# The causal mask of the turned scores: two products on TensorE, or a select by GpSimd on the exponentials

## What is computed

```
q = Q @ WQ + bQ ; k = K @ WK + bK ; v = V @ WV + bV        # 16 heads of 16
scores = einsum('bhqd,bhkd->bhqk', q, k) * SCALE
scores = where(causal, scores, -inf)
probs = softmax(scores, axis=-1)
out = einsum('bhqk,bhkd->bhqd', probs, v) ... @ WO + bO
x = x + out
```

## Time and profile before

| what | value |
|---|---|
| time, median of 3 executions | 732.27 us (730.75 to 733.64) |
| time of the profiled execution | 739.06 us |
| span of the profiled execution | 737.3 us, 11898 instructions |
| busy, share of the span | PE 85%, PEld 70%, DVE 68%, ACT 48%, POOL 45% |
| mean granted TensorE clock | 0.898 of 2.4 GHz |
| chain that ended last, by engine | PE 39%, issue 6%, DVE 5%, POOL 5%, DMA 4%, SP queue 4%, ACT 1% |

### The profile page before, as it was taken

One profiled execution on the slowest core, in us unless ns is written; L12 is line 12 of the kernel. 1 busy time (PEld: TensorE's weight loads), 2 busy tenths in 40 slices (PEclk: granted clock), 3 DMA queues, 4 the chain that ended last, 5 costly groups with the idle time before them and its releaser, 6 DMA issues.

```text
span 737.3 us, 11898 instructions
## 1 busy us (share of the span) xinstructions
PE 626.5 (85%) x4100; PEld 518.1 (70%) x4100; DVE 501.1 (68%) x1066; ACT 350.2 (48%) x683; POOL 333.7 (45%) x322
## 2 busy tenths in 40 slices
PE   3586998997987688889989851799999999999992
PEld 2465887876875554556555531799999999999992
DVE  5687688787696546666657262387888888788841
ACT  4565464662543024352343421356666666666551
POOL 1234424224240032112143367344868677686776
PEclk9798999999999669997788665699999999999997
DMA  9201403775317926556365410704263452521223
GB/s 295 83 3 43 128 29 89 274 203 139 90 44 198 211 64 164 133 141 163 83 162 142 160 38 17 254 22 152 25 170 68 127 153 43 168 31 17 28 29 44
DMA packets 63315, 81.64 MB, mean 111 GB/s; under 512 B 10295, under 2 KB 47938, under 8 KB 63256
## 3 DMA queue, kind: packets, MB, share of 16 engines
q1 hardware_dynamic: 53928, 72.85, 35.2%
q0 software_dynamic: 9216, 7.81, 7.4%
q10 hardware_dynamic: 112, 0.23, 0.1%
HBM read 48.27 MB, written 34.36 MB: 112 GB/s over the span
## 4 chain that ended last, share of the span: by engine, by line
PE 39%; issue 6%; DVE 5%; POOL 5%; DMA 4%; SPq 4%; ACT 1%; POOLq 0%; DVEq 0%; ACTq 0%
PE l_scores L101 13%; PE w_bank L1765 13%; DMA l_lo<-kd 3%; POOL out L1418 2%; PE a_out L1621 2%; SPq L208 2%; PE a_shared L1641 2%; POOL disp L1387 2%; PE l_scores L1699 2%; PE a_turned L1603 1%; PE l_scores L1722 1%; PE a_turned L1589 1%; PE l_scores L261 1%; DVE w_yt L1966 1%; DVE l_nm L275 1%
## 5 line engine op out<-in xcount | busy, mean ns | idle before, releaser
L1954 DVE SCALAR_TENSOR_TENSOR w_v<-w_th,l_scores 128x324 f32<-128x324 f32 x128 | 62.1, 490 | 55.1 <-ACT w_th L1509 53.8
L1509 ACT ACTIVATE w_th<-l_scores 128x324 f32<-128x324 f32 x128 | 56.4, 441 | 84.7 <-PE l_scores L101 83.8
L1405 POOL TENSOR_TENSOR l_lo<-w_v,l_hi 128x324 fp32r<-128x324 f32 x64 | 59.0, 922 | 75.0 <-ACT l_hi L1515 74.8
L1470 ACT ACTIVATE a_pr<-a_turned 128x1024 f32<-128x1024 f32 x48 | 49.1, 1023 | 89.1 <-PE a_turned L1603 87.2
L101 PE MATMUL l_scores<-l_hi,w_w1h 128*128 128x324 f32 x256 | 81.1, 317 | 2.3 <-DVE l_lo L1946 1.2
L1418 POOL DMA_INDIRECT out<-w_y,w_to x48 | 76.3, 1591 | 12.1 <-issue 9.7
L101 PE MATMUL l_scores<-l_lo,w_w1h 128*128 128x324 f32 x256 | 80.6, 315 | 0.0
L101 PE MATMUL l_scores<-l_hi,w_w1l 128*128 128x324 f32 x256 | 80.5, 314 | 0.0
L275 DVE TENSOR_REDUCE l_nm<-l_scores 128x4 f32<-128x1024 f32 (+1 forms) x48 | 58.3, 1215 | 31.7 <-PE l_scores L261 30.9
L1765 PE MATMUL w_bank<-l_hi,w_w2h 128*128 128x324 f32 x256 | 64.5, 323 | 2.2 <-DVE w_yt L1966 1.2
L1515 ACT ACTIVATE l_hi<-w_v 128x324 fp32r<-128x324 f32 x128 | 59.9, 472 | 12.4 <-DVE w_v L1954 11.7
(11 more groups left out here) (253 smaller groups left out, 1587.0 us busy)
## 6 DMA issues: line engine op xcount, KB each, us to landing
w_s<-in_L_ffn_w SPq DMA_DIRECT2D x14, 1024.0 KB, 7.4
l_lo<-kd SPq DMA_DIRECT2D x32, 200.0 KB
l_hi<-qd SPq DMA_DIRECT2D x32, 192.0 KB
disp<-c_blank SPq DMA_DIRECT2D x8, 658.1 KB
w_rows<-disp SPq DMA_DIRECT2D x7, 658.1 KB
kd<-l_qkh SPq DMA_DIRECT2D x16, 256.0 KB, 4.7
vd<-m_vf SPq DMA_DIRECT2D x4, 1024.0 KB, 6.8
qd<-l_qkh SPq DMA_DIRECT2D x16, 256.0 KB, 3.9
```

The source lines that it names most:

```text
L1405: pool.tensor_tensor(hl[:, g % 3, half(1)], v[:, n % 4, :], hh[:, g % 3, half(1)].bitcast(F32), ALU.subtract)\
L1470: act.activation(pr[n % 3][:, :], tbank[:, :], ACT.Exp, scale=SCALE).then_inc(A["exp"], 1)
L1509: act.activation(th[:, n % 2, :], hb[n % 2][:, 0:HALF], ACT.Tanh, scale=0.5).then_inc(F["th"], 1)
L1954: dve.scalar_tensor_tensor(v[:, n % 4, :], th[:, n % 2, :], 1.0, hb[n % 2][:, 0:HALF], ALU.add, ALU.mult).then_inc(F["v"], 1)
```

## The change

`turned_mask` is gone from TensorE and with it 2 products for each of 48 items. `turned(n)` now writes `a_turned` afresh (start=True) and itself waits for the exponential of item n - 1. The exponentials of keys after the query are then not zero, and GpSimd sets them to zero in SBUF: `cut(n)` is an affine select over the diagonal blocks of `pr`, 4 x 128 columns for s = 0 and 1, and 8 x 128 (all of the tile) for s = 2. `weigh(n)` waits for `cut(n)` in place of the exponential. The bias is added by tiles of 256 columns, one behind each of `cut(0)` to `cut(15)`; the additions of `base` become tiles too, one in each of steps 22 to 25 and 34 to 37, and eight at the end. Waits on their semaphores count tiles.

```
@@ -1317,7 +1317,7 @@
                                  .rearrange("(p t) d -> p t d", t=ST)).then_inc(F[f"rows{e % 2}"], 16)
 
                 def store_base(i):
-                    sp.wait_ge(S["base"], i + 1)
+                    sp.wait_ge(S["base"], TPB * (i + 1))
                     sp.dma_start(out[i * BLK:(i + 1) * BLK, :].rearrange("(t p) d -> p t d", p=P),
                                  x_sb[:, i * TPB * D:(i + 1) * TPB * D].rearrange("p (t d) -> p t d", d=D))\
                         .then_inc(S["based"], 16)
@@ -1357,19 +1357,23 @@
 
             @block.gpsimd
             def _(pool):
-                def with_bias(i):
-                    m = x_sb[:, i * TPB * D:(i + 1) * TPB * D].rearrange("p (t d) -> p t d", d=D)
-                    pool.tensor_tensor(m, m, bo[:, :].unsqueeze(1).to_broadcast([P, TPB, D]), ALU.add).then_inc(S["xb"], 1)
+                def with_bias(t):
+                    pool.tensor_tensor(tile(x_sb, t), tile(x_sb, t), bo[:, :], ALU.add).then_inc(S["xb"], 1)
 
                 def power(i):
                     _, own, nt = tiles(i)
                     pool.wait_ge(S["ve"], i + 1)
                     pool.tensor_tensor(rstd[:, own], ve[:, own], c["mhalf"][:, 0:nt], ALU.pow).then_inc(S["rstd"], 1)
 
-                def base(i):
-                    pool.wait_ge(S["x3"], TPB * (i + 1))
-                    m = x_sb[:, i * TPB * D:(i + 1) * TPB * D].rearrange("p (t d) -> p t d", d=D)
-                    pool.tensor_tensor(m, m, x3[:, i * TPB:(i + 1) * TPB, 0:D], ALU.add).then_inc(S["base"], 1)
+                def base(t):
+                    pool.wait_ge(S["x3"], t + 1)
+                    pool.tensor_tensor(tile(x_sb, t), tile(x_sb, t), x3[:, t, 0:D], ALU.add).then_inc(S["base"], 1)
+
+                def cut(n):
+                    pool.wait_ge(A["exp"], n + 1)
+                    own = pr[n % 3][:, :].rearrange("k (m q) -> k m q", m=8 if n % 3 == 2 else 4)[:, :, 0:P]
+                    pool.affine_select(out=own, in_=own, compare_op=ALU.is_ge, fill=0.0, base=0,
+                                       pattern=[[0, own.shape[1]], [1, P]], channel_multiplier=-1).then_inc(A["cut"], 1)
 
                 def divide(g):
                     pool.wait_ge(A["po"], 2 * g + 2)
@@ -1422,15 +1426,18 @@
 
                 pool.iota(x3[:, :, TOK:TOK + 1].bitcast(U32), [[P, NT], [1, 1]], base=0, channel_multiplier=1)\
                     .then_inc(S["xb"], 1)
-                for i in range(NBLK):
-                    with_bias(i)
                 for t in range(END):
+                    if t < NS:
+                        cut(t)
+                    if t < NT:
+                        with_bias(t)
                     if t % 3 == 0 and 1 <= t // 3 <= GR:
                         divide(t // 3 - 1)
                     for i in units(t, "power"):
                         power(i)
-                    if t in BASE:
-                        base(BASE.index(t))
+                    for i, first in enumerate(BASE):
+                        if first <= t < first + TPB:
+                            base(TPB * i + t - first)
                     if t % 6 == 3 and 1 <= t // 6 < FC:
                         low_w1(0, t // 6 - 1)
                     if t % 6 == 0 and 1 <= t // 6 < FC:
@@ -1441,8 +1448,8 @@
                                 scatter(i, n)
                 low_first_w2(FC - 1)
                 low_w1(0, FC - 1)
-                base(NBLK - 2)
-                base(NBLK - 1)
+                for t in range(TPB * (NBLK - 2), NT):
+                    base(t)
                 low(0)
                 for e in range(E):
                     for f in range(FC):
@@ -1580,16 +1587,8 @@
 
                     return [(p, e) for p in range(4) for e in range(2) if s == 2 or p // 2 == s]
 
-                def turned_mask(n):
+                def turned(n):
                     ge(pe, A["exp"], n)
-                    for e in range(2):
-                        bank = tbank[:, e * 4 * P:(e + 1) * 4 * P]
-                        m = 4 if n % 3 == 2 else 2
-                        out = bank.rearrange("k (p q) -> k p q", p=m)[:, :, 0:P]
-                        pe.matmul(out, c["mask"][:, :], c["identb"][:, :].unsqueeze(1).to_broadcast([P, m, P]),
-                                  start=True, stop=False, skip_group_check=True)
-
-                def turned(n):
                     g, s = divmod(n, 3)
                     if s == 0:
                         pe.wait_ge(A[f"m_in{g % 2}"], 32 * (g // 2 + 1))
@@ -1600,14 +1599,14 @@
                         key = slice(P, L) if s == 2 else slice(0, P)
                         w = P if s == 2 else L
                         at = e * 4 * P + (p if s == 2 else p % 2) * w
-                        mm = pe.matmul(tbank[:, at:at + w], kx[rows, p, key], q[rows, p, tok], start=False, stop=True,
+                        mm = pe.matmul(tbank[:, at:at + w], kx[rows, p, key], q[rows, p, tok], start=True, stop=True,
                                        skip_group_check=True)
                     mm.then_inc(A["st"], 1)
 
                 def weigh(n):
                     g, s = divmod(n, 3)
                     b, k = divmod(g, 2)
-                    pe.wait_ge(A["exp"], n + 1)
+                    pe.wait_ge(A["cut"], n + 1)
                     if s == 0:
                         ge(pe, A["po"], 2 * g - 1)
                         pe.wait_ge(A[f"v_in{b % 2}"], 16 * (b // 2 + 1))
@@ -1769,8 +1768,6 @@
 
                 for t in range(END):
                     u = t + LEAD
-                    if t < NS:
-                        turned_mask(t)
                     if u < NS:
                         mask(pe, A, c, lead, u)
                     if t < NS:
@@ -1847,7 +1844,7 @@
                     dve.transpose(ot[:, k, (b % 2) * L:(b % 2 + 1) * L], on[:, :]).then_inc(A["o"], 1)
 
                 def x2(b):
-                    dve.wait_ge(S["xb"], b // 2 + 2)
+                    dve.wait_ge(S["xb"], 2 * b + 3)
                     dve.wait_ge(S["y"], b + 1)
                     m = x_sb[:, 2 * b * D:(2 * b + 2) * D]
                     dve.tensor_tensor(m, y_bank(b)[:, :], m, ALU.add).then_inc(S["x2"], 1)
```

11 lines of the change are left out of this document (4 added, 7 removed).

## The result

| kernel | time, median | ratio to before, 95% interval | mean granted clock |
|---|---|---|---|
| before | 732.48 us (730.75 to 733.64, 4 runs) | | 0.898 (the profiled one, 739.06 us) |
| after | 759.39 us (758.57 to 762.36, 4 runs) | 1.0377 (1.034 to 1.0413) | 0.856 (the profiled one) |

The change makes the kernel 27 us slower. 730.8 us was predicted, with 723.5 to 738 as the range: wrong in sign and in size. The profiled execution of after took 760.13 us, with a span of 758.4. From the fetch of the second expert's rows to the end of the span it is 278.2 us before and 278.0 after, so everything was lost in attention with routing. The execution whose profile serves as before in the rows took 739.06 us and is none of these four.

A forecast was written before the change was run, and what follows sets the result against it. The laying loop, and TensorE when its clock is low, were taken to bound the attention stage in turn. Terms -7.1 + 1.6 + 3.0 + 1.0 = -1.5 us took 739.06 to 737.6 us, carried to 730.8 against the median; range 723.5 to 738.

The forecast's parts named there:

- The additions by tiles ... I count nothing: GpSimd: splitting four additions of 2.36 us into sixteen quarters costs nothing, 0.5 us either way.
- the three rivals: Alternatives: faster, no added clock loss (0.34); slower by clock in the laying loop (0.18); slower by GpSimd's queue (0.08).
- Masks in a full TensorE: -7.1: Attention stage, three stretches where TensorE bounds: masks removed there save 7.1 us (5 to 10); the other 32 count nothing.
- clock falls in two loop turns: +3.0: Laying loop: longer waits for keys lower TensorE's clock, slowing the projection by 1.5 us in each of two turns.
- Rival 2: Laying loop: lower clock slows three turns, costing 9.0 us instead of 3.0; slower, 736.8 us; chance 0.18.
- Shared port: +1.0 (0 to 3): VectorE's small operations on the maxima wait while GpSimd's cuts hold the shared port: 1.0 us more.
- The cuts are hidden: Mid-stage: cuts of 0.7 and 1.2 us finish before `weigh` needs them, if GpSimd is free when the exponential ends.
- a sign of being wrong: Mid-stage: TensorE waiting for cuts for more than 2 us in sum would count against the prediction.
- Rival 3: GpSimd's queue: cuts at upper price (1.17 and 2.35 us) delay steps and the end; about 736.8 us; chance 0.08.
- Tail cut: +1.6: Stage end: the cut before `weigh(46)` queues behind power, low part and scatter, delaying the turned normed rows by 1.6 us.

The follow-up runs named there:

- tiles_only: The kernel before with only the additions of the normed rows by tiles; masks stay products, no cuts: 750.87 us, ratio 1.0295.
- products_gone: The kernel before without the 96 `turned_mask` products, so the turned scores get no causal mask; all additions whole: 736.98 us, ratio 1.01.
- bias_tiles: The kernel before with only the bias added by tiles in the first 16 steps: 731.33 us, ratio 0.9991.
- cut_aside: The kernel before plus 48 GpSimd selects of the cuts' shapes on their own SBUF tile, results awaited by nobody: 736.08 us, ratio 1.0072.
- both_masks: base_whole with the 96 mask products put back on TensorE, overwritten by the turned scores: 736.20 us, ratio 1.0083.
- cut_only: products_gone with the cuts on GpSimd; bias and normed rows added whole: 745.95 us, ratio 1.0226.
- base_whole: The kernel after with the additions of the normed rows whole again; cuts and bias by tiles stay: 744.26 us, ratio 1.024.

## Why the prediction was wrong

- **The step that failed most: "The additions by tiles ... I count nothing".** I asked where GpSimd had room for the additions, and when they began, but not who waits for the last one and what stands behind that waiter. It is SyncE, with the maxima's store and the next keys behind it. The changed wait of `store_base` stood in the diff, and its place ahead of the next group's store in SyncE's loop stood in the kernel. The prediction had this term at 0 with 0.5 us either way. tiles_only priced it at 21 us alone; taking it out of after gave back 15 and 16 us by the medians (10 and 9 by the ratios). None of the three rivals was this one.
- **"Masks in a full TensorE: -7.1", and "clock falls in two loop turns: +3.0".** Taken together these gave -4.1 us; products_gone, which does just this, measured 1.0% or 7 us slower (0.57 to 1.43%, 4 to 10 us). The -7.1 rested on the earlier trace rows: products leave a TensorE that bounds. Those rows are of the execution of 739.06 us. In bias_tiles, nearer to the median, the same 15 us are nearly all at the high clock:

```profile
342.00:357.00 15.00, 14.36 (x152) 8.83 (x150) 12.36 (x39) 5.94 (x8) 2.61 (x4) 0.94 0.46 110
```

  And the granted clock isn't fixed. With fewer products more of the stage runs at 1.2 GHz (0.75 against 0.87 above), and the products left take longer. I had priced only a projection in two turns behind a wait. Rival 2 had the right direction: its -7.1 and +9.0 make +1.9 us for this edit alone, where 7 were measured. That its total of 736.8 us is also the time of products_gone is chance, since it counts 2.6 us for the cuts, which products_gone hasn't. The Trainium skill, page "TensorE: Matmul & The Clock Gate", section "HAM oscillation — how this bites in real kernels", which the prediction cites, says that waits for a DMA bring the clock down, so that the next burst starts slow. The trace of products_gone agrees in one place: TensorE waits 1.86 us for the keys of 333.98, and the straight mask took 0.60 us (two products of 512 columns) before the wait, while the projection of 334.99 behind it took 3.78 us. The projection of 314.95 is slow without a wait in front of it; the clock was at 0.50 from 309 us on, with TensorE busy throughout. The prediction gave low clock of both kinds too little weight.
- **"Shared port: +1.0 (0 to 3)".** The hold-up is there as described, but the term was too small: running the selects costs 0.72% or 5.3 us (3 to 7.6) in cut_aside, if not all of it through these operations. I took half of 0.4 us for each of the turns; measured are 0.31 us (cut_aside) and 0.50 us (both_masks) for each of 16 groups in these two operations alone.
- **"The cuts are hidden".** Nearly right in the middle of the stage: 0.64 and 1.10 us each, and TensorE's wait for them was 2.9 us in six places up to 440 us in after, above the 2 us that the prediction had named as a sign of being wrong. The cuts took 37.9 us in all; the lower bound of that sum is 38 us, not the 36 that the prediction has. Rival 3, GpSimd's queue with cuts at their upper price, fell by the measured lengths. cut_aside shows besides that the selects cost about as much when nobody waits for them.
- **"Tail cut: +1.6".** In after the cut of item 46 stands behind the power, the low part and a scatter, as the earlier trace rows had let expect:

```profile
447.49 1.05 POOL L1391 DMA_INDIRECT disp<-w_x,w_si  x1 [0.18 <-issue]
448.56 0.65 POOL L1375 TENSOR_SCALAR_AFFINE_SELECT a_pr<-a_pr 128x512 f32<-128x512 f32 x1
```

```profile
449.26 1.08 PE L1620 MATMUL a_out<-a_pr,l_lo 128*32 128x256 f32 x8 [3.56 <-POOL a_pr L1375]
```

  `weigh(46)` came 4.5 us after the end of its exponential (444.74) instead of 1.2. The turned rows at 450.28 couldn't have begun before ScalarE had the normed rows at 448.46, so at most 1.8 us of it counts, and the stretch from the last exponential to the last scatter grew from 27.9 to 29.9 us. The prediction's 1.6 is near that.
- **The sum.** By the ratios the missing products (7 us), the running selects (5 us) and the block (21 us alone) make 33 us, more than the 27.6 of after. Taken out of after, the block is worth only 9 to 16 us. One explanation, not tested, is overlap: while a block holds the engines, a late cast or a slow product costs nothing. Without the block the sum is off the other way: cut_only is 16.5 us slower than before by the ratio, where the products and the selects alone make 12.6. So the cuts cost 9 us on top of missing products (by the ratios, with wide intervals) and 5 by themselves. In base_whole TensorE waits 5.8 us for cuts up to 440 us, 3.8 of it at `weigh(46)`, against 1.9 in both_masks; whether that is the rest stays open.

## What to carry to other kernels

When an operation is cut in pieces, follow the wait on its last piece into the queue of whoever waits, and list what stands behind that wait: a store that nobody is in a hurry for can hold up the loads on which everything hangs. Work taken from TensorE in a stage with waits isn't a saving by its length: here 96 products fewer brought the stage's granted clock from 0.87 to 0.75 and made the kernel 1% slower. An instruction on GpSimd can have a price even where nobody waits for its result, as the 48 selects of cut_aside had, 0.72%. And a term that is put at nothing needs the same question as the others: who waits for it?

## What was unexpected in the hardware

- 96 products without effect on the result made the kernel 8 us faster (744.26 to 736.20 us by the medians of base_whole and both_masks), and 84 products issued a second time took back most of what products_gone had lost (736.98 to 732.01 us).
- Extra products only at the waits for keys raised the granted clock (0.73 to 0.80 from 268 to 400 us) without a gain in time (744.26 to 745.20 us).
- A VectorE cast of 16 columns took 210 and 217 ns on average in before and bias_tiles (280 in products_gone), and 459 to 530 ns in cut_aside, both_masks and base_whole, with 48 selects of 0.64 and 1.10 us on GpSimd.
